# Attention output bias added to x by GpSimd instead of a thirteenth TensorE product, coupling factors transposed in two parts, instructions in a new order

## The reference, cut to what matters

```python
x = x + xattn(layernorm(x), ctx, ctx, ...)      # ends in: out @ Wo.T + bo
x = x + ffn(layernorm(x), ...)

def ffn(x):
    gf = global_net(x.mean(axis=1, keepdims=True))        # gc_w1..3
    out = x
    for _ in range(3):
        tf = coupling_net(out)                            # cn_w1..4, one number a row
        coupling = 0.1 + adaptive_range * (0.7 * gf + 0.3 * tf - 0.5) * 2.0
        out = out + coupling * twist(out)
    return out
```

## Time and profile before

| | |
|---|---|
| median of 3 runs | 1368.46 us (1363.71 to 1369.31) |
| profiled execution, its own time | 1367.76 us |
| its span | 1366.0 us |
| PE, DVE, ACT, POOL busy | 91%, 79%, 78%, 46% of the span |
| mean granted TensorE clock | 0.976 of full |

### The profile page before, as it was taken

The page is one execution under the profiler, slowest core; times in us unless marked ns, Lnnn a source line. Parts: engine busy times, 40 slices in busy tenths (PEclk is TensorE's granted clock), DMA queues, the critical chain, the costliest instruction groups (busy, mean ns, idle before and its releaser), DMA issues.

```text
span 1366.0 us, 27848 instructions
## 1 busy us (share of the span) xinstructions
PE 1243.7 (91%) x10392; PEld 865.6 (63%) x10392; DVE 1078.6 (79%) x2125; ACT 1064.5 (78%) x1914; POOL 622.6 (46%) x491
## 2 busy tenths in 40 slices
PE   7867888989999899999999899999999899999984
PEld 5432665658666776658665676658665667657763
DVE  6996459985999679985999769985999759984465
ACT  5743767888878978888878978888878978887665
POOL 1031026571456526562455526572455526462573
PEclk9977999999999999999999999999999999999997
DMA  7466424434335434434335434534335345421001
GB/s 229 139 135 127 99 42 68 93 69 106 75 62 114 91 75 88 101 55 105 71 63 119 72 93 87 104 55 110 71 63 111 68 98 83 79 58 44 28 1 62
DMA packets 319065, 116.54 MB, mean 85 GB/s; under 512 B 301777, under 2 KB 303569, under 8 KB 316882
## 3 DMA queue, kind: packets, MB, share of 16 engines
q1 hardware_dynamic: 318930, 114.76, 40.6%
HBM read 27.58 MB, written 19.53 MB: 34 GB/s over the span
## 4 chain that ended last, share of the span: by engine, by line
PE 51%; DVE 18%; ACT 14%; issue 8%; DMA 6%; POOL 2%; SPq 1%; ACTq 0%; DVEq 0%
PE ps L369 15%; PE ps L269 10%; PE ps L384 10%; PE ps L318 4%; ACT spent L774 4%; DMA x2T<-xr 3%; PE ps L396 3%; DVE xr L1842 3%; PE ps L287 2%; DVE prob L1862 2%; ACT z L846 2%; PE ps L404 2%; DVE xoT L1889 2%; ACT z L854 2%; DVE z L1941 1%
## 5 line engine op out<-in xcount | busy, mean ns | idle before, releaser
L2871 POOL TENSOR_TENSOR h<-z,h 128x512 f16<-128x512 f32 x192 | 241.5, 1264 | 332.2 <-DVE h L1932 332.2
L369 PE MATMUL ps<-x2T,W 128*128 128x256 f16 x3072 | 351.4, 273 | 7.0 <-issue 2.7
L369 PEld LDWEIGHTS ps<-x2T,W 128*128 128x128 f16 x3072 | 297.4, 98 | 56.5 <-issue 11.8
L384 PE MATMUL ps<-h,W 128*128 128x256 f16 x2304 | 276.0, 275 | 7.7 <-POOL h L2871 6.6
L384 PEld LDWEIGHTS ps<-h,W 128*128 128x128 f16 x2304 | 224.2, 99 | 54.6 <-issue 18.1
L2864 POOL TENSOR_TENSOR prob<-prob,rc 128x512 f32<-128x512 f32 x128 | 150.2, 1196 | 161.7 <-DVE rc L1878 161.4
L318 PE MATMUL ps<-WO,xoT 128*128 128x512 f16 x768 | 181.2, 387 | 5.5 <-DVE xoT L1889 4.7
L269 PE MATMUL ps<-xoT,WQ 128*128 128x512 f16 x768 | 173.3, 379 | 4.0 <-issue 3.4
L1932 DVE CAST h<-z 128x512 f16<-128x512 f32 x192 | 101.0, 538 | 62.7 <-ACT z L846 61.6
L1842 DVE TENSOR_TENSOR xr<-ps,xr 128x512 f16<-128x512 f32 x128 | 87.8, 686 | 64.3 <-ACT xr L762 63.1
L318 PEld LDWEIGHTS ps<-WO,xoT 128*128 128x128 f16 x768 | 75.4, 99 | 95.9 <-issue 9.9
(11 more groups left out here) (129 smaller groups left out, 2047.4 us busy)
## 6 DMA issues: line engine op xcount, KB each, us to landing
xin<-x SPq DMA_DIRECT2D x16, 1024.0 KB, 5.7
out<-ot SPq DMA_DIRECT2D x64, 256.0 KB, 2.4
fac<-coup SPq DMA_DIRECT2D x192, 0.5 KB, 2.1
kv_blocks<-kv SPq DMA_DIRECT2D x7, 384.0 KB, 3.0
kvb<-kv_blocks SPq DMA_DIRECT2D x7, 384.0 KB, 3.5
pT<-pr SPq DMA_TRANSPOSE x128, 3.3
wq_s<-wq SPq DMA_DIRECT2D x1, 1024.0 KB, 5.6
wk_s<-wk SPq DMA_DIRECT2D x1, 1024.0 KB, 10.1
```

The lines of the kernel that those rows point to most:

```text
L369: mm = e.matmul(ps[:, BANK_F + L, at * LBLK:(at + 1) * LBLK], w, v, start=(n == 0), stop=(n == 3 * C - 1))
L384: mm = e.matmul(ps[:, BANK_F + L, m * LBLK:(m + 1) * LBLK], w, v, start=(c + m + a == 0), stop=(c == C - 1 and m == C2 - 1 and a == 2))
L2871: e.tensor_tensor(h1[:, L, LO, pair(n)], z[:, L, pair(n)], h1[:, L, HI, pair(n)], ALU.subtract).then_inc(lg[L]["lo1"], 1)
```

## The change

1. The thirteenth matmul of `wo` goes, with BO, `share`, `bo_split` and the waits on them. A new step `xb` on GpSimd adds the bias row to each tile of xin (64 instructions of 128x512), after `xn1` has read that tile and before `res`, which now waits for it too.
2. `coup_turn` has a fourth argument: its first part (4 DMAs, rows 0 and 1) waits for `factors` only, its last part (2 DMAs, row 2) for the last `cc`.
3. The small column tensors become slices of one tensor, ident and bo move, and all five engines' orders are written anew, most of it at the start, in batch 1, and at the end.

```diff
@@ tensor wo @@
-                        e.matmul(ps[:, BANK_M + i % 2], w, v, start=(n == 0), stop=False)
+                        mm = e.matmul(ps[:, BANK_M + i % 2], w, v, start=(n == 0), stop=(n == 3 * C - 1))
                         n += 1
-                e.matmul(ps[:, BANK_M + i % 2], share[:], BO[:], start=False, stop=True).then_inc(sg["wo"], 1)
+                mm.then_inc(sg["wo"], 1)
@@ vector @@
-            def bo_split():
-                e.wait_ge(loaded["bo"], 16)
-                e.tensor_scalar(BO[:], bo_s[:], WSCALE, None, ALU.mult).then_inc(su["bo_split"], 1)
-                e.wait_ge(su["bo_split"], 1)
-                e.scalar_tensor_tensor(BO[KEYS:P], bo_s[KEYS:P], WSCALE, BO[KEYS:P], ALU.mult, ALU.subtract).then_inc(su["bo_split"], 1)
...
             def res(b, t):
                 k, j = divmod(t, TPB)
                 e.wait_ge(sg["wo"], 8 * b + t + 1)
+                e.wait_ge(sg["xb"], 8 * b + t + 1)
@@ gpsimd @@
-                e.memset(share[:], 1.0 / KEYS).then_inc(su["consts"], 1)
...
+            def xb(b, t):
+                k, j = divmod(t, TPB)
+                if b + t == 0:
+                    e.wait_ge(loaded["bo"], 16)
+                e.wait_ge(sg["xn"], tile_of(b, 0, k, j) + 1)
+                e.tensor_tensor(xin[:, slot(b, k), j], xin[:, slot(b, k), j], bo_row[:], ALU.add).then_inc(sg["xb"], 1)
@@ sync @@
-            def coup_turn(p, k, h):
+            def coup_turn(p, k, h, last):
...
-                e.wait_ge(lg[L]["cc"], 3 * u + 3)
-                e.wait_ge(lg[L]["ab"], 3 * u + 3)
+                if last:
+                    e.wait_ge(lg[L]["cc"], 3 * u + 3)
+                else:
+                    e.wait_ge(lg[L]["ab"], 3 * u + 3)
...
-                for n in range(3):
+                for n in (2,) if last else (0, 1):
```

More of the change, by code:

```diff
@@ L2102, in vector_program @@
             aggr(0, 1, 0, 1)
-            res(0, 2); res(0, 3)
+            res(0, 2)
             stats(0, 1, 0, 2)
+            res(0, 3)
             aggr(0, 1, 0, 2)
@@ L2311, in vector_program @@
             stats(2, 0, 1, 3)
-            coef(0, 1, 0)
+            hi1(1, 0, 1, 0, 0)
+            aggr(2, 0, 1, 0); aggr(2, 0, 1, 1); aggr(2, 0, 1, 2); aggr(2, 0, 1, 3)
+            var(2, 0, 1)
+            outs(0, 1, 0, 0)
             xl(2, 0, 0, 3)
             hi1(1, 0, 0, 0, 1)
-            aggr(2, 0, 1, 0); aggr(2, 0, 1, 1); aggr(2, 0, 1, 2); aggr(2, 0, 1, 3)
-            var(2, 0, 1)
-            alph(1)
             nm(2, 0, 1)
             coef(0, 1, 1)
-            outs(0, 1, 0, 0)
@@ L2582, in vector_program @@
             factors(5, 0, 1)
+            hi1(5, 1, 1, 1, 0)
             xl(6, 1, 0, 1)
-            hi1(5, 1, 1, 1, 0)
             res(6, 4)
+            stats(6, 1, 1, 0)
             xl(6, 1, 0, 2)
+            aggr(6, 1, 1, 0)
+            res(6, 5)
             mul(5, 0, 1, 2)
-            stats(6, 1, 1, 0)
-            res(6, 5)
+            stats(6, 1, 1, 1)
             xl(6, 1, 0, 3)
-            aggr(6, 1, 1, 0)
-            pre(5, 0, 1, 2, 0); pre(5, 0, 1, 2, 1)
+            pre(5, 0, 1, 2, 0)
             hi1(5, 1, 1, 1, 1)
-            stats(6, 1, 1, 1)
+            pre(5, 0, 1, 2, 1)
+            aggr(6, 1, 1, 1)
             res(6, 6)
@@ L2749, in vector_program @@
             xl(7, 1, 0, 1)
+            res(7, 4)
             mul(6, 0, 1, 2)
-            res(7, 4)
+            stats(7, 1, 1, 0)
             xl(7, 1, 0, 2)
-            stats(7, 1, 1, 0)
+            aggr(7, 1, 1, 0)
+            pre(6, 0, 1, 2, 0)
             res(7, 5)
+            stats(7, 1, 1, 1)
+            hi1(6, 1, 1, 1, 1)
             xl(7, 1, 0, 3)
-            aggr(7, 1, 1, 0)
-            pre(6, 0, 1, 2, 0); pre(6, 0, 1, 2, 1)
-            hi1(6, 1, 1, 1, 1)
-            stats(7, 1, 1, 1)
+            pre(6, 0, 1, 2, 1)
+            aggr(7, 1, 1, 1)
             res(7, 6)
@@ L2769, in vector_program @@
             var(7, 1, 1)
+            pre(6, 1, 0, 2, 0)
             hi1(6, 0, 1, 2, 0); hi1(6, 0, 1, 2, 1)
[L2771 removed]
             nm(7, 1, 1)
@@ L2809, in vector_program @@
             hi1(7, 0, 1, 1, 0); hi1(7, 0, 1, 1, 1)
+            coef(7, 0, 0)
             mul(7, 1, 0, 1)
@@ L2813, in vector_program @@
             pre(7, 1, 0, 1, 1)
-            hi1(7, 1, 0, 1, 0); hi1(7, 1, 0, 1, 1)
-            coef(7, 0, 0)
-            hi1(7, 1, 1, 0, 1)
+            hi1(7, 1, 0, 1, 0); hi1(7, 1, 0, 1, 1); hi1(7, 1, 1, 0, 1)
             factors(7, 0, 1)
@@ L3014, in gpsimd_program @@
             mulg(7, 1, 0, 2)
-            lo1(7, 0, 1, 2, 1); lo1(7, 1, 0, 2, 0); lo1(7, 1, 0, 2, 1)
+            lo1(7, 0, 1, 2, 1)
+            mulg(7, 1, 1, 2)
+            lo1(7, 1, 0, 2, 0)
             am(7, 1, 1, 0)
-            mulg(7, 1, 1, 2)
+            lo1(7, 1, 0, 2, 1)
             am(7, 1, 1, 1)
```

1667 lines of the change are left out of this document (828 added, 839 removed).

## The result

The changed kernel takes 1377.22 us (median of 8 runs, 1372.28 to 1381.78), the kernel before 1367.09 (8 runs, 1363.71 to 1369.31). The ratio is 1.0079, 95% interval 1.0066 to 1.0092: slower by about 10 us, where 1358, a gain of 10.6 us, was forecast. The profiled execution took 1381.49 us, its span is 1379.6 us, its mean granted clock 0.969 (before: 0.976).

What follows compares the result with a forecast made beforehand. TensorE was taken as nearly full, VectorE equally so in the attention stretch, TensorE alone the bound after it. 4.8 + 2.3 + 1.0 + 2.5 = 10.6 us off 1367.76 leaves 1357.2, so 1358 for the median; range 1349 to 1367.

Steps and rivals of the forecast that it cites:

- The additions' price: 64 GpSimd additions at about 1.2 us each, placed where GpSimd idles; taken as 0 in the sum.
- 0.98 us a push: VectorE's `pre`, with SBUF inputs, takes 1.67 us beside a GpSimd operation against 0.69 alone: 0.98 us more.
- a delay of VectorE is mostly slack; I take 0 for them: First six additions of a batch, 938 to 962 us, VectorE busy 27.75 of 45 us: cost 0.
- the sign that it gave for this case: VectorE's `hi1`, `pre` or `outs` growing by 0.1 us and more would show the port's case has come true.
- shared port: Rival: each batch's last two additions push VectorE's two-input operations by up to 0.98 us; 1381, chance 0.10.
- The product, 4.8 us: Removing the 64 bias products of `wo` from TensorE gains their share on the chain, 4.8 us.
- The chain's 21 pieces: Bias product's pieces on the chain in batches 0, 1, 4 and 6: 0.44 + 20 x 0.22 = 4.8 us.
- the second rival: VectorE's path just behind takes back the 4.8 us; only start and tail remain, 3.5 us: 1365, chance 0.27.
- Order and split, 2.3 + 2.5 us: New order uses a quarter of TensorE's freed off-chain time, 2.3; four small transfers issued before the last `cc`, 2.5 off the tail.
- In the middle batches the same split is hidden: Splitting the coupling transfers gains nothing in middle batches, since `coef` runs while TensorE alone is the bound.
- The 1.0 us of `bo_split`: At the start, dropping `bo_split` from VectorE work on the chain gains 0.34 + 0.69 = 1.0 us.
- The order did it.: Sign of error: middle batches' period changing by more than 1.7 us, the most the removed products hold, would mean the order.

Runs made afterwards that it cites:

- run 3: Changed kernel without the 64 additions and the wait on them, bias left out: 1364.05 us, ratio 0.9982.
- 2: Changed kernel's steps in the old order of all engines, product gone, additions kept, both transfer parts side by side: 1384.67 us, ratio 1.0130.
- run 4: Old order without the thirteenth product and without the additions, bias left out: 1372.99 us, ratio 1.0041.
- 9: Changed kernel with the additions cut from 512 to 64 columns, same places and waits: 1364.27 us, ratio 0.9971.
- run 10: Changed kernel with a GpSimd power of 4 columns in place of each addition, same place and wait, bias left out: 1366.54 us, ratio 0.9975.
- run 15: New order with two-part transfers, no additions, thirteenth product dropped but bias setup kept, bias left out: 1359.70 us, ratio 0.9954.
- run 5: Kernel before with the changed orders and two-part transfers, thirteenth product kept, no additions: 1362.13 us, ratio 0.9969.
- run 7: Changed kernel with the first of the twelve products issued twice, a meaningless thirteenth product: 1381.59 us, ratio 1.0103.
- run 16: Kernel before with the thirteenth product alone dropped, bias left out: 1373.57 us, ratio 1.0050.
- run 11: run 5's kernel with the split undone, both parts of the coupling transfers where the last one stood: 1404.43 us, ratio 1.0262.
- run 6: run 4's kernel with the first of the twelve products issued twice, bias left out: 1366.82 us, ratio 0.9994.
- 12: run 4's kernel with six products on constant weights ahead of each batch's gate product, in TensorE's wait for the means: 1375.63 us, ratio 1.0052.

## Why the prediction was wrong

**Two steps failed.** The forecast had a gain of 10.6 us and nothing for the additions. The runs show a gain of 2.5 us without the additions (run 3), so some 8 us of it never came, and 13.3 us for the additions. Together that is 21 us, the way from the forecast 10.6 us below the kernel before to the measured 10 above it.

**The additions' price was the larger one.** The prediction had the two halves of it: 0.98 us a push on VectorE's operations with SBUF inputs, and the places of the additions. It then wrote of the first six of a batch that there "a delay of VectorE is mostly slack; I take 0 for them", from a busy share of 27.75 of 45 us. The runs show 13.3 us (3 against the changed kernel) and 12 (2 against 4), and that it is the hold on VectorE that costs (9, 10). VectorE's low share there isn't slack: it idles 3.64 us for a transfer, then has a row of nine short dependent steps to do, with the attention half's next steps and the output steps behind them. In batch 5 the second part of that row ran free, the first two steps took 1.05 and 1.03 us more, and an output step 1.0 us more. A hold lasts for what is left of the addition, so it isn't paid by every step: 28.2 us over 64 additions is 0.44 us each.

Of the sign that it gave for this case, `hi1`, `pre` or `outs` longer by 0.1 us and more, one part came in: the second step of `outs` grew from 0.59 to 0.71 us, and with 9.7 us against run 3 it is the largest single piece. `pre` grew from 0.81 to 0.85 us and did so without the additions too (run 3: 0.85), and `hi1` fell. The prediction didn't name `c3f` (5.1 to 9.0 us against run 3), the first `fac` (6.2 to 12.3) and `ab` (5.2 to 8.1), operations on 2 to 4 columns that stand far down in the groups by busy time.

The Trainium skill, SBUF — State Buffer, section Who interferes with whom, says that the instruction which starts later is blocked. The 1.21 us against 0.16 agree with that for the additions. The power of run 10 doesn't fit a hold for as long as any GpSimd instruction on SBUF runs: in batch 5 `c3f` started inside a row of four powers, 0.98 us each, and kept its 0.16 us. The softmax's maximum, whose input is in PSUM, wasn't held. The rival "shared port" (1381, a chance of 0.10) was the nearest to the result and had the right mechanism, but laid it at the last two additions of a batch (1.1 us in all) instead of the first six (20.3 us), so that its number is near by luck.

**The product, 4.8 us.** This is the second step that failed. In the new order the product's removal brought 2.1 us (run 15 against 5), not told from nothing; in the changed kernel a repeated product costs 3 to 4 (run 7); in the old order its removal alone costs 6.8 (run 16). The chain's 21 pieces told how long the products lay on the path, not what stood just behind it. In the new order that was the path through the transposes, ScalarE and VectorE to the means, whose wait took up 6.8 us: the second rival's mechanism.

**Order and split, 2.3 + 2.5 us.** Run 5, which still has `bo_split`, is 4.2 to 5.0 us below before, against 4.8. Right in sum, but in part by luck. The tail alone gave 2.0 for 2.5. The 2.3 us of the order were to come from the time that the removed products free on TensorE, and run 5 has its gain with the products still in: in its profiled execution the six middle batches are 7.6 us shorter, the start up to the second `gz` 2.9 us longer and the tail 2.4 us shorter. "In the middle batches the same split is hidden" isn't borne out for the new order either: with the split undone there, VectorE's waits for the transfers grow from 27.3 us (run 5) to 60.9 (run 11). The 1.0 us of `bo_split` is what run 3's first `gz` suggests, at 161.95 us, 1.3 us earlier than in run 15 (163.28), though the two differ in more of the setup; with the additions, in the changed kernel, it is at 166.63, so that up to 4.7 us of what they cost lie at the start.

**"The order did it."** The prediction named a change of the period by more than 1.7 us as the sign of that. It changed by 1.84. In run 5, with the product and without additions, the first instructions of the global nets of batches 1 and 7 start at 316.53 and 1235.96, a period of 153.2 us; run 3, without both, has 153.2 too (313.3 and 1232.4). So the sign was set wrongly: the order brings the period down by 1.3 us, the removed product does nothing to it, and the additions bring it up by 3.2.

**The granted clock**, which the prediction left out. Each line has the stretch, its length, the busy us of PE, PEld, DVE, ACT and POOL, then the granted clock as a share of 2.4 GHz, the DMA share and GB/s. From the windows of the changed kernel, ahead of and in the global net of batch 5:

```profile
936.00:940.00 4.00, 3.87 (x36) 3.22 (x33) 2.53 (x16) 3.90 (x7) 2.17 (x2) 1.00 0.53 164
940.00:943.00 3.00, 1.68 (x30) 1.50 (x31) 1.09 (x9) 3.00 (x10) 0.00 (x0) 1.00 0.00 0
943.00:946.40 3.40, 3.40 (x20) 2.39 (x18) 2.59 (x13) 3.37 (x7) 0.00 (x0) 0.53 0.02 7
946.40:950.00 3.60, 3.60 (x38) 3.21 (x36) 0.69 (x1) 1.19 (x2) 0.00 (x0) 0.97 0.76 191
```

and of the kernel before, 10 us earlier:

```profile
930.00:933.00 3.00, 2.61 (x39) 2.09 (x37) 1.93 (x18) 3.00 (x10) 0.00 (x0) 1.00 0.10 1
933.00:936.40 3.40, 3.40 (x34) 3.05 (x32) 2.79 (x16) 3.37 (x8) 1.01 (x1) 1.00 0.24 82
```

Behind a stretch in which TensorE was busy 1.68 of 3 us the clock is at the lower level, 1.2 of 2.4 GHz, for some 3.4 us; before, behind 2.61 of 3, it isn't. From 200 us to the tail the changed kernel has six such stretches in its profiled execution and the kernel before one. By the means, 0.969 against 0.976, there are 2 x 0.007 x 1377 = 19 us more at half the clock, which cost at most half of that, 10 us. How much they do cost isn't settled. For a share of it speaks run 6, where time and clock came back together. In run 4's kernel the four executions with a clock of 0.975 or more took 1364.2 to 1368.1 us and the eight others 1370.1 to 1382.9, which goes together but doesn't say which of the two makes the other. Against the clock as the whole cause speaks that run 3, with the same 0.969, is 13 us faster: the additions' price isn't the clock's. A repeated product in the changed kernel (7) and the filling in run 4's (12) didn't bring the clock back, so they tell nothing of its price.

**What stays open** is why the old order gets slower with a product less in each tile (4, 16) and recovers with a useless one (6). The clock fell from 0.977 to 0.972 in run 16, which is 2 x 0.005 x 1374 = 14 us more at half speed and costs at most 7 us: by that bound it could be all of the 6.8, but a kernel with the work of before and a lowered clock, or the reverse, wasn't to be had. The other candidate, that the orders of five engines no longer fit each other when one is earlier, is argued only.

## What to carry to other kernels

An addition moved to an idle GpSimd isn't free when its operands lie in SBUF: lay its place beside VectorE's timeline, and look for short operations with SBUF operands that start while it runs, above all behind a late transfer. Each can be held until the addition ends, here up to 1.05 us, and 0.44 us of VectorE's time for each addition on average. A low busy share of an engine is no slack if it waits there for a transfer and then has dependent steps to run. Work taken from a bound engine is worth what the next path leaves: change that work's amount alone, down and up, before an edit is built on it. Here 64 products less changed the time by +7 us in one order and -2 in the other, and 128 more cost 19 and 31.

## What was not expected of the hardware

A VectorE operation of 4 columns, 0.16 us by itself, took 1.21 us beside a GpSimd addition of 512 columns, but 0.16 beside a GpSimd power that was 0.98 us long: a GpSimd instruction's being busy isn't enough for the hold. The two differ in the operation and in how much they move, and no run parts these. TensorE's granted clock fell to its half level in six stretches of about 3.4 us between 200 us and the tail of the changed kernel, whose TensorE is busy 90% of the span. In the old order the median clock fell from 0.977 to 0.972 with the product dropped (run 16); in the new order it is 0.971 with the product and without it (runs 5 and 15). It differed between executions of one kernel too (0.968 to 0.980 in run 4's), together with their times.
